# Gated cross-attention block: attention scores of three heads at once into three banks, one bank for transposed probabilities, four small loads moved to GpSimd's queue, and a new hand-written order of every engine

## The chip, the cores and the metric

One core of a Trainium2 chip runs the whole program. The metric is the device time of one execution in microseconds (us). The engines are TensorE (PE, with its weight loads shown apart as PEld), VectorE (DVE), ScalarE (ACT), GpSimd (POOL) and SyncE (SP), which only issues transfers.

## What is computed

Eight sequences of 256 rows by 512 channels go through a gated cross-attention and a gated feed-forward block. The attention has 16 heads of 32 channels, float32 scores, softmax and values; its two outer projections work on rows quantised to integers, and the feed-forward part on rows rounded to an 8-bit float.

```python
x = x + jnp.tanh(g_xattn[0]) * xattn(_layernorm(x, axis=-1), ctx_2048, mask, wq, bq, wk, bk, wv, bv, wo, bo)
...
# xattn: q = w8a8_linear(x, wq, bq); k = cond @ wk.T + bk; v = cond @ wv.T + bv
scores = jnp.einsum('bhnd,bhld->bhnl', q, k) * inv_sqrt_d + mask[:, None]
attn = jax.nn.softmax(scores, axis=-1)
o = jnp.einsum('bhnl,bhld->bhnd', attn, v)
return _w8a8_linear(o, wo, bo)
...
# ffn, on the layer-normed x: g, u = 8-bit linears with w_gate, w_up (1408 x 512)
t = jax.nn.silu(g) * u
y = 8-bit linear of t with w_down; the result is x + tanh(g_ffn[0]) * y
```

## The kernel before

The program is a software pipeline over eight batches. In each step three generations are worked at once: the attention of the last batch (heads 4 to 15 in slots 0 to 11, the first four heads of the new batch in slots 12 to 15), the projections K, V and Q of the new batch, and the output projection and feed-forward of the batch before. A step has 16 slots, one per head. Step 0 (`first_step_order`) and step 1 (`second_step_order`) also prepare the weights: wq, wk, wv, wo, and 15 "units" of the feed-forward weights, each scaled (`scale_unit`, DVE), lifted (`mag_unit`, ACT: an absolute value and a scaled copy), rounded (`round_unit`, DVE), transposed (`turn_unit`, PE) and copied out (`copy_unit`, ACT). Steps 2 to 7 are alike (`steady_step_order`). The tail (`tail_order`) ends the last attention (blocks `k`) and has two feed-forwards to do, the second of them (blocks `e`) on buffers of its own.

Every engine runs its own list of blocks in order; the lists are written out by hand, and semaphores hold the engines together. So what comes behind a block that waits on an engine waits too.

The path of one head: `score_pair` (L797) on PE writes the scores of two heads into `S_BANK[0]` and `S_BANK[1]`, one 512-column PSUM bank each. A head has 32 channels, so its matmuls use 32 rows of the array, each head of a pair another 32, and the two heads' matmuls alternate (L804 to L807). `head_mask` (L1292, DVE) adds the mask and takes the row's extremum into `prob` (two buffers); `head_exp` (L603, ACT) exponentiates in place; `head_turn` (L865, PE) transposes the 256 x 256 probabilities of the head of the slot before into one of two `T_BANK`s; `head_probT` (L617, ACT) copies that to `probT`; and after four heads `group_pv` (L900, PE) multiplies with V into bank O. `head_turn` waits for the exponentials (`exped`) and for the copy of the head two before (`turned_out`). `score_pair` waits until both heads before it are masked (L803). The eight calls per step score slots in pairs.

At the turn of a step: `oqT_turn` (L876, PE) transposes the rounded attention output, `oqT_low` (L1285, DVE) and `oqT_high` (L563, ACT) copy it out of PSUM, and `y_project` (L1003, PE) needs both. `v_evac(12)` (L1329 and `v_out`, L1219, DVE) moves the second half of V out of bank O (`V_BANK[1]`), and `group_pv(13)` waits for it (`v_ready`) since it writes that bank.

Loads: SP issues wq, wk, x, the context, wv, then two gates, two bias rows, wo, and the bias columns bk and bq (L303 to L312), and then the mask. ACT's `gate_tanhs` (L549) waits for all four small loads (`small_loaded` at 64), and everything behind it on ACT with it. GpSimd gathers gate and up rows by index (`load_unit`, L328).

## Time and profile before

| | us |
|---|---|
| median of 3 runs | 603.62 |
| lowest and highest of them | 601.6, 651.39 |
| the profiled execution | 601.54 |
| its span, first to last instruction | 599.8 |

The rows below are from the profiled execution. They are its page (a summary by engine and by group of instructions) and answers of its trace: timelines, tables of stretches, and lists of waits. "L807" is line 807 of the kernel. Matmuls are pipelined, and their ends are modelled: what a group of matmuls costs is read from its start to the start of the next group. DVE and ACT instructions overlap by up to 0.1 us in the timelines in the same way.

### The profile page before, as it was taken

The page shows a single profiled execution, that of the slowest core. Times are in us where ns is not written, and L with a number is a line of the kernel's source. Part 1 is how long each engine was busy: PE and PEld are TensorE (multiplying, and loading weights), DVE is VectorE, ACT ScalarE, POOL GpSimd, SP SyncE. Part 2 cuts the span into 40 slices and gives each one's busy share as a digit, 9 for nine tenths or more (in the row PEclk, how much of TensorE's full clock was granted, in tenths as well). Part 3 has the DMA queues.
Part 4 walks back from the last instruction along what each step waited for, and adds up shares of the span by engine and source line. Part 5 has one row for each costly group of instructions (what it writes and reads, how often), then busy time and mean ns, then how long its engine had stood idle before and what let it go on. Part 6 is the DMA issues. An engine that isn't in the chain of part 4 may idle for free.

```text
span 599.8 us, 10833 instructions
## 1 busy us (share of the span) xinstructions
PE 524.7 (87%) x3456; PEld 331.9 (55%) x3456; DVE 514.4 (86%) x1286; ACT 475.6 (79%) x1156; POOL 225.6 (38%) x208
## 2 busy tenths in 40 slices
PE   1867897899999999999999999999999998876834
PEld 1755475556755675577557655765576555433311
DVE  5798997678899989998999799979997996699794
ACT  5298998989888889888988898889788987783351
POOL 3223343002472447244715471546164613361430
PEclk9886997989999999999999999999999998796888
DMA  9912433010101010101010101010100000000000
GB/s 315 342 45 54 122 107 105 18 54 2 37 0 55 36 37 2 54 36 37 2 54 37 37 0 55 37 36 1 54 37 1 1 2 36 0 2 0 35 1 36
DMA packets 15240, 28.75 MB, mean 48 GB/s; under 512 B 3792, under 2 KB 5840, under 8 KB 15184
## 3 DMA queue, kind: packets, MB, share of 16 engines
q1 hardware_dynamic: 10560, 16.65, 8.1%
q0 software_dynamic: 3200, 11.41, 5.7%
q8 instruction: 28, 0.46, 0.3%
q10 hardware_dynamic: 1424, 0.01, 0.1%
q14 instruction: 28, 0.23, 0.1%
HBM read 23.87 MB, written 4.19 MB: 47 GB/s over the span
## 4 chain that ended last, share of the span: by engine, by line
PE 55%; DVE 23%; issue 10%; ACT 5%; SPq 3%; DMA 2%; DVEq 0%; POOL 0%; POOLq 0%; ACTq 0%
PE bank_s L807 9%; PE bank_t L872 7%; PE bank_u L827 5%; PE bank_g L827 5%; PE bank_a L814 4%; PE bank_g L814 4%; DVE prob L1299 3%; PE bank_o L914 3%; DVE q L1194 3%; PE bank_a L838 3%; DVE t_sb L1189 2%; DMA bq_col<-in_L_xattn_bq_dram 2%; DVE t_sb L1233 2%; DVE ts L1484 2%; PE bank_g L1048 2%
## 5 line engine op out<-in xcount | busy, mean ns | idle before, releaser
L612 ACT ACTIVATE prob<-prob,neg_max 128x256 f32<-128x256 f32 x256 | 127.2, 503 | 2.8 <-DVE neg_max L1299 2.8
L1299 DVE CUSTOM_DVE_ANT_0 prob<-bank_s,mask_sb 128x256 f32<-128x256 f32 x256 | 96.4, 420 | 19.9 <-PE bank_t L872 9.2
L623 ACT ACTIVATE probT<-bank_t 128x512 f32<-128x512 f32 x128 | 73.2, 588 | 20.2 <-PE bank_t L872 17.3
L397 POOL TENSOR_TENSOR up<-up,wgu_scale 128x512 f32<-128x512 f32 (+1 forms) x42 | 54.8, 1305 | 88.9 <-ACT up L592 88.9
L872 PE MATMUL bank_t<-ident,prob 128*128 128x128 f32 x512 | 78.3, 281 | 3.0 <-ACT prob L612 2.6
L807 PE MATMUL bank_s<-kf,qf 32*128 32x256 f32 x512 | 74.3, 408 | 6.9 <-DVE neg_max L1299 4.7
L872 PEld LDWEIGHTS bank_t<-ident,prob 128*128 128x128 f32 x512 | 59.2, 143 | 30.1 <-issue 19.7
L807 PEld LDWEIGHTS bank_s<-kf,qf 32*128 32x128 f32 x512 | 44.6, 188 | 31.0 <-issue 19.6
L407 POOL TENSOR_TENSOR up<-gate,up 128x512 f32<-128x512 f32 (+1 forms) x42 | 54.4, 1295 | 4.1 <-DVE gate L1359 1.4
L412 POOL TENSOR_TENSOR x<-x,y 128x512 f32<-128x512 f32 x14 | 19.6, 1399 | 96.6 <-DVE y L1497 96.6
L612 ACT ACTIVATION_READ_ACCUMULATOR prob<-prob,neg_max 128x1 f32 x256 | 50.1, 196 | 0.0
L827 PE MATMUL bank_u<-wguT,x2T 128*128 128x512 bf16 (+1 forms) x168 | 41.2, 369 | 0.0
L827 PE MATMUL bank_g<-wguT,x2T 128*128 128x512 bf16 (+1 forms) x168 | 40.6, 364 | 0.0
L1359 DVE SCALAR_TENSOR_TENSOR gate<-bank_g,x2s,wgu_scale 128x512 f32<-128x512 f32 (+1 forms) x42 | 29.5, 703 | 11.6 <-PE bank_g L827 11.6
L914 PE MATMUL bank_o<-probT,v_sb 128*32 128x256 f32 x512 | 36.0, 401 | 3.1 <-ACT probT L623 3.0
L513 ACT ACTIVATE mag<-t_sb,ts 128x512 f32<-128x512 f32 (+1 forms) x42 | 28.6, 681 | 11.1 <-DVE ts L1489 5.6
L592 ACT ACTIVATE up<-bank_u,x2s 128x512 f32<-128x512 f32 (+1 forms) x42 | 27.0, 643 | 6.4 <-PE bank_u L827 5.5
L1233 DVE SCALAR_TENSOR_TENSOR t_sb<-th,up 128x512 f32<-128x512 f32 (+1 forms) x42 | 30.5, 727 | 1.2 <-POOL up L407 1.2
L814 PE MATMUL bank_a<-c_in,wkT 128*128 128x256 f32 x128 | 31.4, 390 | 0.0
L679 ACT ACTIVATE th<-gate 128x512 f32<-128x512 f32 (+1 forms) x42 | 24.8, 589 | 8.3 <-DVE gate L1359 7.7
L820 PE MATMUL bank_a<-wvT,c_in 128*128 128x512 f32 x64 | 31.2, 610 | 0.0
L820 PE MATMUL bank_o<-wvT,c_in 128*128 128x512 f32 x64 | 30.5, 602 | 0.0
(258 smaller groups left out, 1213.8 us busy)
## 6 DMA issues: line engine op xcount, KB each, us to landing
x_in<-in_x_dram SPq DMA_DIRECT2D x8, 512.0 KB
c_in<-in_ctx_dram SPq DMA_DIRECT2D x8, 512.0 KB, 3.4
out_dram<-x POOLq DMA_DIRECT2D x7, 512.0 KB, 3.3
mask_sb<-in_mask_BxSxS_ff_dram SPq DMA_DIRECT2D x8, 256.0 KB, 3.7
t_sb<-in_L_ffn_w_down_dram SPq DMA_DIRECT2D x2, 704.0 KB, 5.3
t_sb<-in_L_ffn_w_down_dram POOLq DMA_DIRECT2D x2, 704.0 KB
kf<-in_L_xattn_wq_dram SPq DMA_DIRECT2D x1, 1024.0 KB, 8.9
probT<-in_L_xattn_wk_dram SPq DMA_DIRECT2D x1, 1024.0 KB, 11.0
```

The costliest lines, as they stand in the source:

```text
L397: pool.tensor_tensor(up[:, c % 2, 0:w], up[:, c % 2, 0:w], wu_scale[:, off:off + w], ALU.mult).then_inc(f["u_scaled"], 1)
L407: pool.tensor_tensor(up[:, c % 2, 0:w], gate[:, c % 2, 0:w], up[:, c % 2, 0:w], ALU.mult).then_inc(f["gu_ready"], 1)
L612: ins = act.activation(prob[:, head_par, t, :], prob[:, head_par, t, :], ACT.Exp, bias=neg_max[:, head_par, t:t + 1], scale=-1.0, accum_ou ...
L623: act.activation(probT[:, (slot + 3) % 4, :, :].rearrange("p a b -> p (a b)"), T_BANK[(slot + 1) % 2][:, :], ACT.Copy).then_inc(s["turned_ ...
L807: ins = pe.matmul(S_BANK[(slot + i) % 2][:, t * L:(t + 1) * L], qf[r:r + 32, hb, c, t * P:(t + 1) * P], kf[r:r + 32, hb, c, :], start=(t = ...
L814: ins = pe.matmul(k_bank(W, hf)[:, o * L:(o + 1) * L], wkT[:, c, (2 * hf + o) * P:(2 * hf + o + 1) * P], ctxT(c), start=(c == 0), stop=(c ...
L820: ins = pe.matmul(V_BANK[lt][:, :], ctxT(c)[:, lt * P:(lt + 1) * P], wvT[:, c, :], start=(c == 0), stop=(c == CC - 1))
L827: ins = pe.matmul(bk_[:, 0:w], x2T[:, c, t * P:(t + 1) * P], wT[:, c, off:off + w], start=(c == 0), stop=(c == CC - 1))
L872: ins = pe.transpose(T_BANK[1 - hp][:, lc * N + t * P:lc * N + (t + 1) * P], prob[:, 1 - hp, t, lc * P:(lc + 1) * P], ident[:, :])
L914: ins = pe.matmul(O_BANK[32 * j:32 * j + 32, 0:N], v_sb[:, 1 - par, lc, (4 * g + j) * Dh:(4 * g + j + 1) * Dh], probT[:, j, lc, :], start= ...
L1233: dve.scalar_tensor_tensor(t_sb[t][:, off:off + w], th[:, 0:w], 1.0, up[:, c % 2, 0:w], ALU.add, ALU.mult).then_inc(f["t_ready"], 1)
L1299: ins = dve.tensor_tensor_reduce(prob[:, hp, t, :], S_BANK[hp][:, t * L:(t + 1) * L], mask_sb[:, hb, t, :], -1.0, 3.4e38, ALU.add, ALU.min ...
```

## The change

- `S_BANK` has three banks and `T_BANK` one. `score_group` scores three heads with interleaved matmuls at four places of a step (called from slots 2, 5, 8 and 15) and two at two places (slots 11 and 13): six groups for 16 heads where there were eight.
- `head_turn` waits for the copy of the head right before it, as there is one bank.
- SP no longer issues the two gates, bk and bq; wo follows wv at once. GpSimd issues those four ahead of its first gather.
- For units 7, 9, 11 and 13 the scaled copy of `mag_unit` goes from ACT to DVE (two `tensor_scalar` in `round_unit`).
- The order lists of PE, ACT and DVE are rewritten in all steps, GpSimd's in steps 0 and 1 and in the tail. Among them, in the steady step: on PE no score group stands between `oqT_turn` and `y_project`, but `head_turn(1)`; `group_pv(13)` follows `first_score(11)` at once; on ACT `head_exp(0)` and `head_probT(0)` stand ahead of `oqT_high`; on DVE `v_evac(12)` stands behind `head_mask(12)`.

```diff
-        S_BANK, T_BANK, O_BANK, A_BANK, G_BANK, U_BANK = bank[0:2], bank[2:4], bank[4], bank[5], bank[6], bank[7]
+        S_BANK, T_BANK, O_BANK, A_BANK, G_BANK, U_BANK = (bank[0], bank[1], bank[3]), bank[2], bank[4], bank[5], bank[6], bank[7]
+        SCORED_FROM = {2: 3, 5: 3, 8: 3, 11: 2, 13: 2, 15: 3}
+        SCORE_BANK = [S_BANK[slot % 3] for slot in range(12)] + [S_BANK[0], S_BANK[1], S_BANK[2], S_BANK[0]]
...
-            return (S_BANK + T_BANK)[e % 4]
+            return bank[e % 4]
...
+        DVE_UNITS = (7, 9, 11, 13)
...
                     load8("v", wv)
-                    for n, g in enumerate((g_xattn, g_ffn)):
-                        sp.dma_start(gates[:, n:n + 1], g.rearrange("(a n) -> a n", a=1).to_broadcast([P, 1])).then_inc(s["small_loaded"], 16)
+                    load8("o", wo)
                     sp.dma_start(bo_row[:, :], bo.rearrange("(a n) -> a n", a=1).to_broadcast([P, C])).then_inc(s["row_loaded"], 16)
                     sp.dma_start(bv_row[:, :], bv.rearrange("(a n) -> a n", a=1).to_broadcast([P, C])).then_inc(s["row_loaded"], 16)
-                    load8("o", wo)
-                    sp.dma_start(bk_col[:, :], bk.rearrange("(c p) -> p c", p=P), allow_slow_non_contiguous=True).then_inc(s["small_loaded"], 16)
-                    sp.dma_start(bq_col[:, :], bq.rearrange("(c p) -> p c", p=P), allow_slow_non_contiguous=True).then_inc(s["small_loaded"], 16)
                     sp.wait_ge(s["wq_loaded"], 16)
...
+            for n, g in enumerate((g_xattn, g_ffn)):
+                pool.dma_start(gates[:, n:n + 1], g.rearrange("(a n) -> a n", a=1).to_broadcast([P, 1])).then_inc(s["small_loaded"], 16)
+            pool.dma_start(bk_col[:, :], bk.rearrange("(c p) -> p c", p=P), allow_slow_non_contiguous=True).then_inc(s["small_loaded"], 16)
+            pool.dma_start(bq_col[:, :], bq.rearrange("(c p) -> p c", p=P), allow_slow_non_contiguous=True).then_inc(s["small_loaded"], 16)
             pool.wait_ge(s["index_loaded"], 16)
             load_unit(2)
             load_unit(3)
@@ -419,10 +422,10 @@
                     load, x_var, x2_add, x2_var, x_plus_bias, up_scale, gate_up, out_add, out_store)
 
             def first_step_order(k):
-                k.load(4); k.x_var(0); k.load(6); k.x_plus_bias(4); k.load(8); k.load(12); k.load(10); k.load(14)
+                k.x_var(0); k.load(6); k.load(4); k.load(8); k.x_plus_bias(4); k.load(10); k.load(14); k.load(12)
 
             def second_step_order(k):
-                k.load(0); k.load(4); k.x_plus_bias(4); k.x_var(0); k.load(2); k.load(8); k.load(6)
+                k.load(0); k.load(4); k.x_plus_bias(4); k.load(2); k.x_var(0); k.load(6); k.load(8)
...
                     for n in range(2):
-                        act.activation(m[:, n * C:(n + 1) * C], raw[:, n * C:(n + 1) * C], ACT.Abs, scale=wf_r[:, k % 3, 1, n:n + 1])
-                    for n in range(2):
+                        ins = act.activation(m[:, n * C:(n + 1) * C], raw[:, n * C:(n + 1) * C], ACT.Abs, scale=wf_r[:, k % 3, 1, n:n + 1])
+                    for n in range(0 if k in DVE_UNITS else 2):
                         ins = act.activation(raw[:, n * C:(n + 1) * C], raw[:, n * C:(n + 1) * C], ACT.Copy, scale=wf_r[:, k % 3, 0, n:n + 1])
...
-                                   T_BANK[(slot + 1) % 2][:, :], ACT.Copy).then_inc(s["turned_out"], 1)
+                                   T_BANK[:, :], ACT.Copy).then_inc(s["turned_out"], 1)
...
             def first_step_order(k):
...
+                k.unit_mag_0(0); k.unit_mag(2); k.pro_round_q(0); k.x_centre(0); k.pro_k(0); k.ctxT_copy(0)
+                k.ctxT_copy(1); k.pro_round_o(3); k.unit_mag(4); k.gate_tanhs(2); k.k_out_0(3); k.k_out_1(4)
+                k.x_round(2); k.pro_v(2); k.unit_copy(3); k.wo_scaled(6); k.unit_mag(6); k.xT_high(6); k.unit_copy(5)
+                k.unit_copy(7); k.unit_mag(8); k.unit_copy(9); k.unit_mag(10); k.q_high(7); k.unit_copy(11)
+                k.q_high(8); k.unit_mag(12); k.head_exp(12); k.head_exp(13); k.head_probT(13); k.unit_copy(13)
+                k.unit_mag(14); k.head_exp(14); k.head_probT(14); k.head_exp(15); k.unit_copy(15); k.head_probT(15)
 
...
+                k.head_exp(0); k.head_probT(0); k.oqT_high(0); k.head_exp(1); k.ctxT_copy(0); k.x_centre(0)
+                k.group_oT(1); k.head_probT(1); k.ctxT_copy(1); k.head_exp(2); k.head_probT(2); k.x_round(2)
+                k.head_probT(3); k.head_exp(3); k.head_probT(4); k.k_out_0(3); k.head_exp(4); k.x2_mag_0(3)
+                k.x2_mag_1(3); k.group_oT(5); k.head_exp(5); k.head_probT(5); k.k_out_1(4); k.head_probT(6)
...
+                k.head_exp(10); k.head_probT(10); k.gate_tanh(11); k.head_exp(11); k.head_probT(11); k.head_probT(12)
+                k.tT_high(12); k.t_mag_0(12); k.head_exp(12); k.t_mag_1(12); k.t_mag_2(13); k.head_exp(13)
+                k.head_probT(13); k.group_oT(13); k.tT_high(14); k.head_probT(14); k.head_exp(14); k.head_exp(15)
+                k.head_probT(15); k.o_round(15)
...
-                def score_pair(slot):
+                def score_group(slot, count):
 
                     n = 16 * b + slot - LEAD
                     h = (slot + 4) % SLOTS
                     hb = 1 - par if slot < LEAD else par
 
-                    need(pe, s["masked"], n)
+                    need(pe, s["masked"], n - 1 if slot in (LEAD, LEAD + 2) else n)
                     for t in range(NT):
-                        for i in range(2):
+                        for i in range(count):
                             c, r = (h + i) // 4, 32 * ((h + i) % 4)
-                            ins = pe.matmul(S_BANK[(slot + i) % 2][:, t * L:(t + 1) * L], qf[r:r + 32, hb, c, t * P:(t + 1) * P],
+                            ins = pe.matmul(SCORE_BANK[(slot + i) % SLOTS][:, t * L:(t + 1) * L], qf[r:r + 32, hb, c, t * P:(t + 1) * P],
                                             kf[r:r + 32, hb, c, :], start=(t == 0), stop=True, skip_group_check=True)
                             if t == NT - 1:
                                 ins.then_inc(s["scored"], 1)
...
-                    need(pe, s["turned_out"], n - 2)
+                    need(pe, s["turned_out"], n - 1)
                     for lc in range(LC):
                         for t in range(NT):
-                            ins = pe.transpose(T_BANK[1 - hp][:, lc * N + t * P:lc * N + (t + 1) * P],
+                            ins = pe.transpose(T_BANK[:, lc * N + t * P:lc * N + (t + 1) * P],
                                                prob[:, 1 - hp, t, lc * P:(lc + 1) * P], ident[:, :])
                     ins.then_inc(s["turned_ps"], 1)
...
-                k.head_score(15)
+                k.pro_turn_k(0); k.pro_turn_q(0); k.ctxT_turn(0); k.ctxT_turn(1); k.k_project_even(2)
+                k.k_project_even(3); k.unit_turn(2); k.k_project_odd(2); k.k_project_odd(3); k.pro_turn_v(1)
+                k.wo_scale_turn(5); k.xT_turn(4); k.unit_turn(4); k.pro_turn_o(4); k.xT_turn(5); k.sx_turn(6)
+                k.unit_turn(6); k.q_project_0(6); k.unit_turn(8); k.q_project_1(7); k.unit_turn(10)
+                k.v_project_low(10); k.v_project_high(10); k.first_score(11); k.v_project_low(11); k.head_turn(13)
+                k.unit_turn(12); k.head_score(13); k.head_turn(14); k.v_project_high(11); k.head_score(15)
+                k.unit_turn(14); k.head_turn(15)
...
-                k.head_turn(0); k.ctxT_turn(0); k.oqT_turn(0); k.head_score(1); k.y_project(0); k.head_turn(1)
-                k.head_turn(2); k.ctxT_turn(1); k.group_pv(1); k.k_project_even(2); k.head_score(3); k.head_turn(3)
-                k.k_project_odd(2); k.head_turn(4); k.k_project_even(3); k.xT_turn(4); k.group_pv(5)
-                k.k_project_odd(3); k.xT_turn(5); k.head_turn(5); k.head_score(5); k.x2T_turn(5); k.sx_turn(6)
-                k.head_turn(6); k.up_project(5); k.gate_project(5); k.q_project_0(6); k.up_project(6)
-                k.gate_project(6); k.head_turn(7); k.up_project(7); k.head_score(7); k.gate_project(7); k.head_turn(8)
-                k.up_project(8); k.q_project_1(7); k.gate_project(8); k.up_project(9); k.head_score(9); k.head_turn(9)
-                k.gate_project(9); k.group_pv(9); k.up_project(10); k.v_project_low(10); k.gate_project(10)
-                k.v_project_high(10); k.head_turn(10); k.v_project_low(11); k.first_score(11); k.head_turn(11)
-                k.head_turn(12); k.tT_turn(11); k.v_project_high(11); k.down_project_low(12); k.head_score(13)
-                k.down_project_high(12); k.group_pv(13); k.head_turn(13); k.tT_turn(13); k.head_turn(14); k.o_turn(14)
-                k.down_project_low(14); k.down_project_high(14); k.head_turn(15); k.head_score(15)
+                k.head_turn(0); k.ctxT_turn(0); k.oqT_turn(0); k.head_turn(1); k.y_project(0); k.group_pv(1)
+                k.ctxT_turn(1); k.head_score(2); k.head_turn(2); k.k_project_even(2); k.head_turn(3)
+                k.k_project_odd(2); k.head_turn(4); k.k_project_odd(3); k.xT_turn(4); k.k_project_even(3)
+                k.group_pv(5); k.head_turn(5); k.head_score(5); k.sx_turn(6); k.x2T_turn(5); k.head_turn(6)
+                k.xT_turn(5); k.up_project(5); k.gate_project(5); k.up_project(6); k.head_turn(7); k.q_project_0(6)
+                k.gate_project(6); k.up_project(7); k.q_project_1(7); k.gate_project(7); k.head_turn(8)
+                k.up_project(8); k.gate_project(8); k.head_score(8); k.head_turn(9); k.group_pv(9); k.up_project(9)
+                k.gate_project(9); k.v_project_low(10); k.v_project_high(10); k.up_project(10); k.gate_project(10)
+                k.v_project_low(11); k.head_turn(10); k.v_project_high(11); k.head_turn(11); k.tT_turn(11)
+                k.head_turn(12); k.first_score(11); k.group_pv(13); k.down_project_low(12); k.down_project_high(12)
...
+                if k in DVE_UNITS:
+                    for n in range(2):
+                        dve.tensor_scalar(raw[:, n * C:(n + 1) * C], raw[:, n * C:(n + 1) * C], wf_r[:, k % 3, 0, n:n + 1], None,
+                                          ALU.mult).then_inc(s["wf_lifted"], 1)
+                    dve.wait_ge(s["wf_lifted"], 2 * DVE_UNITS.index(k) + 2)
...
             def first_step_order(k):
...
+                k.pro_int_q(0); k.x_scales(2); k.pro_q(0); k.pro_scale_o(2); k.unit_scale(2); k.unit_round(3)
+                k.unit_scale(4); k.unit_round(5); k.pro_v(2); k.pro_int_o(4); k.bias_scale(3); k.xT_low(5); k.pro_o(5)
+                k.sx_copy(7); k.unit_scale(6); k.unit_round(7); k.q_scale_0(7); k.unit_scale(8); k.unit_round(9)
+                k.q_scale_1(8); k.unit_scale(10); k.unit_round(11); k.v_evac(11); k.head_mask(12); k.head_mask(13)
+                k.unit_round(13); k.unit_scale(12); k.head_mask(14); k.head_mask(15); k.unit_scale(14); k.v_evac(12)
+                k.unit_round(15)
...
             def steady_step_order(k):
                 k.head_mask(0); k.head_mask(1); k.oqT_low(0); k.x_stats(0); k.y_scale(1); k.head_mask(2)
...
+                k.x_scales(2); k.head_mask(3); k.x2_stats(2); k.x2_centre(3); k.head_mask(4); k.x2_max(3); k.xT_low(5)
+                k.head_mask(5); k.x2_sum_0(4); k.x2_sub_0(4); k.x2_sum_1(4); k.x2_sub_1(4); k.x2T_copy(5)
+                k.head_mask(6); k.gate_scale(6); k.head_mask(7); k.sx_copy(7); k.head_mask(8); k.q_scale_0(7)
+                k.gate_scale(7); k.t_mul(7); k.q_scale_1(8); k.gate_scale(8); k.t_mul(8); k.gate_scale(9); k.t_mul(9)
+                k.head_mask(9); k.t_scales(9); k.t_mul(10); k.gate_scale(10); k.t_sum_0(10); k.head_mask(10)
+                k.t_sub_0(10); k.t_sum_1(10); k.t_mul(11); k.t_sub_1(10); k.v_evac(11); k.gate_scale(11)
+                k.t_sum_2(11); k.head_mask(11); k.t_mul_last(11); k.t_sub_2(11); k.t_scales(11); k.head_mask(12)
+                k.v_evac(12); k.tT_low(12); k.t_sum_0(12); k.head_mask(13); k.t_sub_0(12); k.t_sum_1(12)
                 k.t_sub_1(12); k.t_sum_2(13); k.y2_scale(13); k.t_sub_2(13); k.head_mask(14); k.tT_low(14)
```

## Rows read from the trace of the kernel before

**Rows 1.** Parts 1 and 5 of the page: busy us and share; then busy, mean ns.

```profile
PE 524.7 (87%) x3456; PEld 331.9 (55%) x3456; DVE 514.4 (86%) x1286; ACT 475.6 (79%) x1156; POOL 225.6 (38%) x208
...
L623 ACT ACTIVATE probT<-bank_t 128x512 f32<-128x512 f32 x128 | 73.2, 588 | 20.2 <-PE bank_t L872 17.3
```

**Rows 2.** Table of stretches: window, length, then busy us of each engine, clock, DMA.

```profile
0.00:31.16 31.16, 14.85 (x85) 13.29 (x85) 20.94 (x36) 13.13 (x17) 8.32 (x18) 0.95 0.90 320
31.16:74.70 43.54, 31.43 (x189) 22.53 (x191) 39.15 (x76) 40.09 (x79) 13.83 (x12) 0.80 0.26 73
74.70:139.84 65.14, 55.39 (x397) 39.39 (x393) 51.69 (x138) 59.69 (x147) 12.01 (x12) 0.92 0.21 65
...
317.42:376.61 59.19, 58.96 (x403) 37.02 (x401) 53.80 (x148) 51.40 (x133) 26.36 (x24) 1.00 0.09 32
...
540.00:600.00 60.00, 33.80 (x152) 14.55 (x152) 46.63 (x82) 19.15 (x33) 14.54 (x12) 0.78 0.05 18
```

**Rows 3.** Timeline of PE in one steady step: start us, us, line, tile, count.

```profile
283.40 0.81 PE L827 MATMUL bank_u<-wguT,x2T 128*128 128x384 bf16 x4
284.14 1.13 PE L807 MATMUL bank_s<-kf,qf 32*128 32x256 f32 x8
285.20 0.82 PE L827 MATMUL bank_g<-wguT,x2T 128*128 128x384 bf16 x4
285.87 0.60 PE L872 MATMUL bank_t<-ident,prob 128*128 128x128 f32 x4
...
292.51 1.07 PE L914 MATMUL bank_o<-probT,v_sb 128*32 128x256 f32 x16
293.51 0.82 PE L827 MATMUL bank_u<-wguT,x2T 128*128 128x384 bf16 x4
```

**Rows 4.** Timeline of all engines at the turn of a steady step.

```profile
316.00 1.34 ACT L638 ACTIVATE rows<-rows,os 128x512 f32<-128x512 f32 x2 [1.12 <-DVE os L1352]
...
318.41 1.13 PE L807 MATMUL bank_s<-kf,qf 32*128 32x256 f32 x8
...
318.52 0.69 DVE L1290 TENSOR_SCALAR turned<-bank_g 128x512 bf16<-128x512 f32 x1 [0.36 <-PE bank_u L884]
319.01 0.50 ACT L612 ACTIVATE prob<-prob,neg_max 128x256 f32<-128x256 f32 x1
...
319.48 1.04 PE L1008 MATMUL bank_u<-woT,turned 128*128 128x512 bf16 x4
```

**Rows 5.** Timeline of DVE: a head's mask, and V leaving bank O.

```profile
303.73 0.42 DVE L1299 CUSTOM_DVE_ANT_0 prob<-bank_s,mask_sb 128x256 f32<-128x256 f32 x1
...
307.65 0.68 DVE L1223 TENSOR_TENSOR v_sb<-bank_o,bv_row 128x512 f32<-128x512 f32 x1
```

**Rows 6.** Timeline of ACT, and of DVE, in step 0: the two late loads.

```profile
31.16 0.20 ACT L551 ACTIVATE tgate<-gates 128x2 f32<-128x2 f32 x1 [10.68 <-DMA bq_col<-in_L_xattn_bq_dram]
30.26 2.29 DVE L1132 TENSOR_REDUCE w_max<-raw_o 128x4 f32<-128x2048 f32 x1 [3.21 <-DMA raw_o<-in_L_xattn_wo_dram]
```

**Rows 7.** DMA issues of the page: KB each, us from issue to landing.

```profile
qf<-in_L_xattn_wv_dram SPq DMA_DIRECT2D x1, 1024.0 KB, 15.4
raw_o<-in_L_xattn_wo_dram SPq DMA_DIRECT2D x1, 1024.0 KB, 18.1
```

**Rows 8.** Timeline of SP's queue: when it issued.

```profile
5.18 1.46 SPq L286 DMA_DIRECT2D qf<-in_L_xattn_wv_dram  x1
...
12.17 0.52 SPq L286 DMA_DIRECT2D raw_o<-in_L_xattn_wo_dram  x1
...
17.23 4.79 SPq L312 DMA_DIRECT2D bq_col<-in_L_xattn_bq_dram  x1
```

**Rows 9.** Groups of ACT's and DVE's unit work: busy us, mean ns.

```profile
L1420 DVE TENSOR_SCALAR rows<-x,mv 128x512 f32<-128x512 f32 x14 | 6.2, 484 | 0.2
...
L476 ACT ACTIVATE t_sb<-t_sb,wf_r 128x512 f32<-128x512 f32 x8 | 5.4, 732 | 0.0
```

**Rows 10.** What ACT waited for from 31.2 to 139.9 us: total, times, longest.

```profile
ACT wguT L488 <- PE bank_g L787: 3.9, 4, 2.1
```

186 lines of the change are left out of this document (76 added, 110 removed).

## The prediction, made before the changed kernel ran

> **What bounds the kernel now.** I read the page first: PE is busy 87% of the span, DVE 86%, ACT 79% [rows 1]. Those are averages, so the table of stretches comes next [rows 2]. It shows three regimes. Steps 0 and 1, up to 139.84 us, are different: from 31.16 us on ACT is busy 40.09 of 43.54 and then 59.69 of 65.14 us, more than any other engine, so ACT carries them, and before that it stands still for 10.68 us until bq_col has landed [rows 2, 6]. From 540 us on DVE is busiest (46.63 of 60.00), in chains of short dependent work.
>
> I split 599.8 us into 139.84 (steps 0 and 1), 355.1 (six steps of 59.18) and 104.9 (the tail), and sum against the profiled execution, 601.54. The median shown, 603.62, is 2 us above it, the lowest run, 601.6, at it.
>
> **Steady steps: what the third head saves.** A pair costs 1.06 us from its start at 284.14 to the next group at 285.20 [rows 3]. Two heads of two halves each, in two passes per matmul, are eight records in four rounds. That the work of several heads runs side by side is seen in the product with V: sixteen records, four heads wide, take 1.00 us (292.51 to 293.51), no more than eight records of two. So I cost a group of three like a pair, 1.06; the far end is that the third head runs by itself, another 1.06 at most, since a lone head has the same four rounds. Six groups for eight save 2 x 1.06 = 2.12. The block in front of a group is a little longer too: up_project of 384 columns takes 0.74 ahead of the scores, the same form 0.67 elsewhere (285.20 to 285.87), so two groups fewer give another 0.14. Sum: -2.26 a step. The Trainium skill, TensorEngine Tiling (Array Packing), Key Properties, says that changing the tiling mode drains TensorE and that different tiles may run in parallel; this trace agrees (0.07 us in front, pairs at 1.06), and without that drain the saving would be 2.12.
>
> **Steady steps: what the new order takes back.** I followed the new lists block by block with the old durations. Three places stand out.
> (a) `oqT_turn` to `y_project`. Before, a score group (318.41 to 319.48) filled exactly the time that DVE (318.52 + 0.69) and ACT needed to copy the transposed rows [rows 4]. Now only `head_turn(1)`, about 0.45, stands there, and ACT does `head_exp(0)` and `head_probT(0)` ahead of `oqT_high`: from the end of `o_round` at 317.34, 2 x 0.49 for the exponentials and 0.48 for the copy end at 318.9, `oqT_high` at 319.5, so `y_project` starts at 319.6, where it did. PE loses the score's 1.06 less 0.45: +0.6.
> (b) `group_pv(13)` needs `v_evac(12)`, which now stands behind `head_mask(12)` on DVE, which needs `first_score(11)`, the block right in front of `group_pv(13)` on PE. PE must stand still for the mask (2 x 0.35), the evacuation (0.61 net of overlap) and two handovers of 0.1 [rows 5]: +1.5 in each step, whatever else is on time. Down projection, `o_turn` and the next step are queued behind it.
> (c) `head_score(2)` waits for `head_mask(2)`, behind `y_scale`: +0.15.
> Against that, today's list too holds waits too short for the lists of waits, and where PE stands anyway, these cost nothing more; I estimate -0.5. Net: -2.26 + 0.6 + 1.5 + 0.15 - 0.5 = -0.5 to -0.7. I take **-0.6 a step, -3.6 for six**. Ends: -2.26 (nothing lost, -13.6) and +0.5 (the lost time twice as long as I see, +3).
>
> **One T bank.** A turn now waits for the copy of the head before it. The copy takes 0.588 [rows 1], with handovers 0.75. In the steady list PE has at least the eleven transposes of `tT_turn` between any two turns and nearly always over 1 us, and ACT's list has each copy near its turn. I cost it 0.1 a step, inside the sum above; if half of the turns were uncovered by 0.7, it would be +5.6 a step.
>
> **Steps 0 and 1.** (d) The stall. `gate_tanhs` waited for bq_col until 31.16 [rows 6]; SP issued it at 17.23, as its last [rows 8]. Now GpSimd issues the four from about 2 us. If each took the longest time that SP needed for one, 4.79, the last would be issued at 16.4, and with the 13.9 from issue to the end of ACT's wait, land at 30.3. On ACT's new list `gate_tanhs` comes behind `pro_round_o` and `unit_mag(4)`, about 32, so that wait is gone even so. GpSimd's gathers of units 2 and 3 would then start at 21 at the latest, and are first read at 27: covered. What is late next is wo: `pro_round_o` now stands ahead. wo was issued at 12.17 and took 18.1, landing at 30.26 [rows 6 to 8]. It is now issued at 6.7, behind wv, which landed at 5.18 + 15.4 = 20.6; 1 MB at the stretch's 320 GB/s [rows 2] is 3.3 more, so 24 to 25 with the gathers beside it. DVE's maximum (2.29 + 0.4) ends at 27.6, and ACT then goes on with the same work done as at 31.16: **-3.5**. The Trainium skill, DMA: Bandwidth & Descriptors, Issuing engine by pattern, calls the sync and scalar paths generally faster for simple loads; no run here shows GpSimd's time for such a load, and by the bounds above it changes nothing.
> (e) The offload. Four units of two copies, 0.61 net of overlap each (0.73 shown [rows 9]), leave ACT: -4.9 on the engine that carries these steps. DVE gets eight of 0.40 net (0.484), 3.2 us; it is busy 39.15 of 43.54 and 51.69 of 65.14, so the second stretch has 13 us for them [rows 2]. **-4.9**.
> (f) Order. After 31.2 ACT still waited, mostly for `unit_turn` and `copy_unit` (3.9 [rows 10]). Walking the new lists I find `o_round` of step 1 ending at about 128 for 139.8, which is 3.3 more than (d) and (e). A walk forgets small waits; I take half: **-1.6**.
> Together -10; bounds -3.5 (the offload only moves the bound to DVE) and -12.
>
> **Tail.** `up_project(5)` comes some 2 us earlier by my walk, but `group_pv(13)` and `o_turn` some 2 later, as they stand behind all gate and up projections, and from 540 DVE's own list sets the end. 0, within +-3.
>
> **Sum.** 601.5 - 3.6 - 10.0 + 0 = 588.
>
> **The rivals.**
> 1. The steady step keeps all that the third head saves: PE is as full as before, and (a) to (c) do not show. For it: PE's 58.96 of 59.19. Against: (b) is forced by the lists. 601.5 - 13.6 - 10 = 578.
> 2. Only the offload or only the early wo counts in steps 0 and 1, and the steady step is a draw: DVE, 2 x 3.2 us nearer to full, or the later `ctxT_turn` becomes the bound. For it: DVE is within 1 us of ACT until 74.7 us. 601.5 - 4.5 + 1 = 598.
> 3. On the other side: the third head doesn't ride along. Price: 1.06 for each of four groups of three, +4.2 a step on PE, which has no slack, some 1 us of it absorbed: -0.6 + 3.2 = +2.6 a step, and 4 in the other steps: 601.5 - 10 + 16 + 4 = 612. It decides from 1.6 us for a group of three, where all gains are eaten. For it: the trace has no three row groups at once. Against: four column groups at 1.00.
> 4. The lone T bank at the price above: +33, 621. Against: no turn stands next to another in the steady list of PE.
>
> **Chances.** Forecast (588, own range 582 to 595) 0.50; rival 1 0.20; rival 2 0.18; rival 3 0.07; rival 4 0.05. The range of 576 to 600 holds the first three but for their outer ends, and about 0.8. A measurement here can tell about 2%, 12 us: faster by over that means below 591.5 against 603.6: all of rival 1 and 0.42 of the forecast's 0.50, 0.62. Slower by over 2%, above 615: rival 4 and part of rival 3, 0.08. Between: 0.30.
>
> **What would show it.** Right: 12 records of scores in about 1.07 us from start to start; a PE gap of 1.3 to 1.6 us ahead of `group_pv(13)` in each steady step with DVE's mask and V in it; steady steps of 58.3 to 58.8 us; ACT with no wait at `tgate`, one for wo's scale ending at 27 to 28; `oqT_turn` of step 2 near 130. Wrong: groups of three over 1.3 us; steps under 57.3 or over 59.2; probabilities' turns waiting for ACT's copy over 1 us a step; bq_col landing after 32; step 2 starting after 136.

## The result, and the profile after

The changed kernel is slower: 616.33 us (median of 4 runs) against 604.91 for the kernel before on the same chips, a ratio of 1.0218 (95% interval 1.0155 to 1.0282). One run of the kernel before, a slow one of 651.39 us, is in its median but not in the ratio. The change is slower beyond the noise; whether by more than 2%, the interval leaves open. The profiled execution spans 614.5 us, the one before 599.8. In the same three parts as in the prediction (cut at the start of `oqT_turn` on TensorE):

| us | before | after | difference | forecast |
|---|---|---|---|---|
| steps 0 and 1 | 139.84 | 137.10 | -2.7 | -10.0 |
| six steady steps | 355.1 (59.18 each) | 367.4 (60.5, then 61.3 to 61.7) | +12.3 | -3.6 |
| tail | 104.9 | 110.0 | +5.1 | 0 |

Part 1 of the page after, and two groups of part 5. They answer to [rows 1]: TensorE is busy 7 us less, but 6.6 of that is in steps 0 and 1 (101.7 to 95.1), where its mean granted clock was 0.97 and not 0.89; in the six steady steps, with twelve groups of scores fewer, it is busy only 1.7 us less (353.5 to 351.8). ScalarE's copy of the turned probabilities waits 37.7 us for TensorE (17.3 before).

```profile
PE 517.3 (84%) x3456; PEld 322.2 (52%) x3456; DVE 519.3 (85%) x1294; ACT 473.9 (77%) x1148; POOL 225.7 (37%) x212
...
L626 ACT ACTIVATE probT<-bank_t 128x512 f32<-128x512 f32 x128 | 75.9, 593 | 38.8 <-PE bank_t L875 37.7
...
L917 PE MATMUL bank_o<-probT,v_sb 128*32 128x256 f32 x512 | 39.3, 430 | 14.7 <-DVE v_sb L1229 9.9
```

The last row has the loss in it: the product with V waited 9.9 us for V to leave its bank, and its matmuls have a mean of 430 ns (401 before). The table of stretches after (columns as in [rows 2]): steps 0 and 1, then a steady step.

```profile
31.16:74.70 43.54, 33.71 (x229) 24.60 (x228) 36.82 (x71) 35.18 (x71) 13.83 (x14) 0.96 0.39 116
74.70:137.10 62.40, 50.69 (x400) 36.51 (x398) 55.98 (x146) 58.80 (x145) 12.34 (x12) 0.96 0.20 62
...
320.26:381.92 61.66, 58.90 (x403) 36.28 (x401) 54.22 (x148) 51.82 (x133) 26.16 (x24) 0.97 0.09 31
```

The steady step has the busy time of [rows 2] (58.90 against 58.96) though TensorE has less to do, and a granted clock of 0.97, not 1.00. The timeline of TensorE after shows why: first a group of three, then the place ahead of `group_pv(13)`.

```profile
325.95 0.48 PE L810 MATMUL bank_s<-kf,qf 32*128 32x256 f32 x2
...
327.02 0.66 PE L875 MATMUL bank_t<-ident,prob 128*128 128x128 f32 x4
...
364.98 1.13 PE L810 MATMUL bank_s<-kf,qf 32*128 32x256 f32 x8
367.77 1.85 PE L917 MATMUL bank_o<-probT,v_sb 128*32 128x256 f32 x16 [1.65 <-DVE v_sb L1229]
369.56 2.32 PE L1051 MATMUL bank_g<-wdT,turned 128*128 128x512 bf16 x6
371.72 1.24 PE L1057 MATMUL bank_g<-wdT,turned 128*128 128x512 bf16 x5
...
376.73 1.46 PE L1051 MATMUL bank_g<-wdT,turned 128*128 128x512 bf16 x6
378.02 0.60 PE L875 MATMUL bank_t<-ident,prob 128*128 128x128 f32 x4
```

Three heads take 1.07 us from start to start (325.95 to 327.02), as a pair does [rows 3]: the third head rides. Ahead of V TensorE stands still for 1.65 us, and what follows is slow: the product takes 1.79 (367.77 to 369.56; 1.00 in [rows 3]), the down projection 2.16 (to 371.72; 1.29 for the same six matmuls at 376.73). The table of stretches shows the clock of that place: at the 2.4 GHz level up to the pause, near the 1.2 GHz level (0.52 of full in the mean; 0.50 from 368.5 to 371.3) behind it.

```profile
364.00:367.70 3.70, 2.12 (x21) 1.42 (x18) 3.02 (x10) 2.89 (x8) 0.00 (x0) 1.00 0.59 215
367.80:371.20 3.40, 3.40 (x20) 1.25 (x21) 3.37 (x9) 2.68 (x6) 0.00 (x0) 0.52 0.02 5
```

The pause stands in all six steady steps, 1.65 us each time, but the low clock in five of them. In the first steady step the same pause was followed by work at full clock:

```profile
185.36 1.07 PE L917 MATMUL bank_o<-probT,v_sb 128*32 128x256 f32 x16 [1.65 <-DVE v_sb L1229]
186.36 1.47 PE L1051 MATMUL bank_g<-wdT,turned 128*128 128x512 bf16 x6
```

VectorE's timeline at the pause: the mask waits for the scores that stand right ahead of the pause, and V leaves its bank behind it.

```profile
366.24 0.42 DVE L1305 CUSTOM_DVE_ANT_0 prob<-bank_s,mask_sb 128x256 f32<-128x256 f32 x1 [0.61 <-PE bank_s L810]
...
366.94 0.69 DVE L1229 TENSOR_TENSOR v_sb<-bank_o,bv_row 128x512 f32<-128x512 f32 x1
```

And the turn of the step, TensorE and ScalarE after: the place of [rows 4]. `head_turn(1)` waits 0.75 us for ScalarE's copy; `y_project` (L1011) then starts at 322.54, when ScalarE's other copy has ended (321.82 + 0.58).

```profile
321.82 0.58 ACT L571 ACTIVATE turned<-bank_u 128x512 bf16<-128x512 f32 x1
322.05 0.63 PE L875 MATMUL bank_t<-ident,prob 128*128 128x128 f32 x4 [0.75 <-ACT probT L626]
322.54 1.02 PE L1011 MATMUL bank_u<-woT,turned 128*128 128x512 bf16 x4
```

The books of a steady step with the low clock in it, from start to start of TensorE's blocks: 59.2 before; -2.1 for two groups fewer; +1.65 pause ahead of V; +0.79 and +0.87 slow work behind it; +0.75 at the turn of the step; +0.1 elsewhere: 61.3. The first steady step has no slow work and took 60.5; some 0.7 of it is not explained by these terms, and a_v_first's first steady step is 0.7 longer than its typical one, too.

### The profile page after: what moved, and what is told of

Its sections match the earlier page's. It is cut to its first block, busy times and chain, and to the rows that moved or that the text cites. A ratio compares the mean times of both kernels' runs of the same rounds, so it can differ in the third digit from the quotient of the medians.

```text
span 614.5 us, 10833 instructions
## 1 busy us (share of the span) xinstructions
PE 517.3 (84%) x3456; PEld 322.2 (52%) x3456; DVE 519.3 (85%) x1294; ACT 473.9 (77%) x1148; POOL 225.7 (37%) x212
## 4 chain that ended last, share of the span: by engine, by line
PE 57%; ACT 14%; DVE 12%; issue 10%; POOL 3%; DMA 3%; SPq 0%; POOLq 0%; ACTq 0%; DVEq 0%
PE bank_t L875 8%; PE bank_s L810 6%; PE bank_o L917 5%; PE bank_u L830 5%; PE bank_a L817 4%; ACT prob L615 4%; PE bank_g L817 3%; PE bank_g L830 3%; PE bank_g L1051 3%; ACT probT L626 2%; DVE prob L1305 2%; ACT t_sb L517 2%; PE bank_a L841 2%; PE bank_g L1057 2%; DMA kf<-in_L_xattn_wq_dram 2%
## 5 line engine op out<-in xcount | busy, mean ns | idle before, releaser
L626 ACT ACTIVATE probT<-bank_t 128x512 f32<-128x512 f32 x128 | 75.9, 593 | 38.8 <-PE bank_t L875 37.7
L875 PE MATMUL bank_t<-ident,prob 128*128 128x128 f32 x512 | 82.9, 286 | 15.4 <-ACT probT L626 13.7
L400 POOL TENSOR_TENSOR up<-up,wgu_scale 128x512 f32<-128x512 f32 (+1 forms) x42 | 51.1, 1216 | 87.2 <-ACT up L595 87.2
L1305 DVE CUSTOM_DVE_ANT_0 prob<-bank_s,mask_sb 128x256 f32<-128x256 f32 x176 | 66.7, 420 | 10.4 <-PE bank_s L810 4.1
L410 POOL TENSOR_TENSOR up<-gate,up 128x512 f32<-128x512 f32 (+1 forms) x42 | 57.4, 1366 | 5.3 <-DVE gate L1365 2.5
L810 PE MATMUL bank_s<-kf,qf 32*128 32x256 f32 x352 | 55.2, 406 | 1.8 <-DVE neg_max L1305 1.8
L917 PE MATMUL bank_o<-probT,v_sb 128*32 128x256 f32 x512 | 39.3, 430 | 14.7 <-DVE v_sb L1229 9.9
L810 PE MATMUL bank_t<-kf,qf 32*128 32x256 f32 x160 | 46.0, 407 | 0.0
L810 PEld LDWEIGHTS bank_s<-kf,qf 32*128 32x128 f32 x352 | 33.1, 187 | 16.2 <-issue 10.8
L1305 DVE CUSTOM_DVE_ANT_0 prob<-bank_t,mask_sb 128x256 f32<-128x256 f32 x80 | 30.6, 420 | 4.9 <-PE bank_t L875 4.3
L917 PEld LDWEIGHTS bank_o<-probT,v_sb 128*32 128x32 f32 x512 | 15.2, 117 | 30.8 <-issue 20.7
```

The costliest lines, as they stand in the source:

```text
L400: pool.tensor_tensor(up[:, c % 2, 0:w], up[:, c % 2, 0:w], wu_scale[:, off:off + w], ALU.mult).then_inc(f["u_scaled"], 1)
L410: pool.tensor_tensor(up[:, c % 2, 0:w], gate[:, c % 2, 0:w], up[:, c % 2, 0:w], ALU.mult).then_inc(f["gu_ready"], 1)
L626: act.activation(probT[:, (slot + 3) % 4, :, :].rearrange("p a b -> p (a b)"), T_BANK[:, :], ACT.Copy).then_inc(s["turned_out"], 1)
L810: ins = pe.matmul(SCORE_BANK[(slot + i) % SLOTS][:, t * L:(t + 1) * L], qf[r:r + 32, hb, c, t * P:(t + 1) * P], kf[r:r + 32, hb, c, :], st ...
L875: ins = pe.transpose(T_BANK[:, lc * N + t * P:lc * N + (t + 1) * P], prob[:, 1 - hp, t, lc * P:(lc + 1) * P], ident[:, :])
L917: ins = pe.matmul(O_BANK[32 * j:32 * j + 32, 0:N], v_sb[:, 1 - par, lc, (4 * g + j) * Dh:(4 * g + j + 1) * Dh], probT[:, j, lc, :], start= ...
```

## The experiments

The starts of `oqT_turn` cut every run into the same parts. The ratio is to the kernel before, on the same chip. The same lists and loads of steps 0 and 1 gave 135.2 to 137.1 in four kernels (after, a_v_first, a_filled, a_v_half), and 133.8 to 135.7 in five with late small loads. The kernel before spreads more: b_half has its lists, loads and code in steps 0 and 1 unchanged and took 136.2 where before took 139.84. In b_half the granted clock from 31.16 to 74.7 us was 0.88, in before 0.80:

```profile
31.16:74.70 43.54, 29.63 (x189) 20.74 (x191) 39.77 (x76) 39.83 (x79) 14.38 (x12) 0.88 0.26 75
```

So a difference to before of under 4 us in that column is no finding by itself; there the ratios of the whole, from many runs, decide. "Typical" is the middle of the steady steps: the first two of a_v_first took 59.9 and 60.4, and one of a_tlow 61.2.

| kernel | ratio, 95% interval | steps 0, 1 | a steady step (typical) |
|---|---|---|---|
| after | 1.0218 (1.0155, 1.0282) | 137.1 | 61.3 |
| a_v_first | 1.0015 (0.9984, 1.0045) | 137.0 | 59.1 |
| a_filled | 1.0098 (1.0063, 1.0133) | 135.2 | 59.7 |
| a_turn | 1.0472 (1.0423, 1.0521) | 137.1 | 63.0 |
| mixed | 1.0067 (1.0020, 1.0114) | 137.8 | 60.0 |
| a_v_half | 0.9968 (0.9924, 1.0012) | 135.7 | 59.2 |
| b_half | 0.9939 (0.9894, 0.9983) | 136.2 | 58.8 |
| a_best | 0.9968 (0.9927, 1.0009) | 134.3 | 59.2 |
| a_tlow | 1.0056 (1.0007, 1.0105) | 135.7 | 59.5 |
| a_tlow_half | 0.9972 (0.9917, 1.0026) | 134.4 | 59.2 |
| a_mask13b | 1.0250 (1.0206, 1.0293) | 133.8 | 61.5 |
| a_mask13 | 1.0294 (1.0252, 1.0335) | 134.2 | 61.5 |
| b_loads | 0.9964 (0.9933, 0.9996) | 138.6 | 59.2 |
| b_loads_late | 0.9928 (0.9895, 0.9960) | 135.0 | 59.2 |
| b_offload | 1.0050 (1.0011, 1.0089) | 143.7 | 59.2 |
| a_first_old | 1.0270 (1.0216, 1.0323) | 138.3 | 61.3 |
| a_second_old | 1.0552 (1.0505, 1.0599) | 156.1 | 61.3 |
| a_no_offload | 1.0339 (1.0280, 1.0398) | 143.8 | 61.3 |

**The pause and its clock.** a_v_first moves one block of the changed kernel:

```diff
-k.t_scales(11); k.head_mask(12); k.v_evac(12); k.tT_low(12)
+k.t_scales(11); k.v_evac(12); k.head_mask(12); k.tT_low(12)
```

> The changed kernel with one block of VectorE moved in the steady steps: V's second half leaves bank O (v_evac(12)) ahead of the mask of slot 12 instead of behind it. In the changed kernel TensorE stands still for 1.65 to 1.8 us ahead of group_pv(13) in each steady step, and for 3.4 us behind that its granted clock is 0.50, so that the product with V takes 1.79 to 1.85 instead of 1.00 and the first down projection 2.16 instead of 1.29. Theory 1 (this wait and the clock that falls behind it are the main loss of the steady steps): the gap falls to about 0.4 us, the clock stays at 1.00, and a step goes from 61.3 to 58.0-58.4 us; six steps give back 18 us: 596-599. Theory 2 (only the wait counts; the work behind it waits for something else anyway): 59.7 a step, -10 us, 605-607. Theory 3 (VectorE's masks and the exponentials of slots 12 and 13 are what is late): 61 a step, no change.

59.1 a step: between theories 1 and 2. The timeline of TensorE in a_v_first at the same place:

```profile
303.39 1.07 PE L917 MATMUL bank_o<-probT,v_sb 128*32 128x256 f32 x16 [0.24 <-DVE v_sb L1229]
304.71 1.47 PE L1051 MATMUL bank_g<-wdT,turned 128*128 128x512 bf16 x6 [0.25 <-DVE turned L1333]
...
308.25 0.66 PE L875 MATMUL bank_t<-ident,prob 128*128 128x128 f32 x4
309.62 0.28 PE L1044 MATMUL bank_g<-ident_h,q 128*128 128x128 bf16 x2 [0.71 <-DVE q L1200]
```

The granted clock is 1.00 in all six steady steps. Of the 3.3 us of pause and slow clock 0.24 is left; another 0.25 + 0.71 come back where TensorE now waits for VectorE's next results. That leaves 2.1 of a gain, and 2.2 were measured. a_filled leaves the pause's cause and only fills it:

```diff
+def warm(slot):
+    for i in range(14):
+        pe.transpose(S_BANK[2][:, (i % 4) * P:(i % 4 + 1) * P], ident[:, :], ident[:, :])
...
-k.first_score(11); k.group_pv(13)
+k.first_score(11); k.warm(13); k.group_pv(13)
```

> The changed kernel with 14 more transposes of a constant (about 1.5 us of TensorE work whose result nobody reads), put into the gap ahead of group_pv(13) in each steady step. Nothing else is moved, and the wait for V stays. If the fallen clock has a price of its own, group_pv(13) and the down projection behind it run at full speed although TensorE got more work: 0.8 + 0.87 = -1.6 us a step, 59.6-59.8, and 606-608 for the whole. If the low clock costs nothing (what stands behind waits for other engines anyway), the step stays at 61.3 and the time at 616; if the extra work doesn't fit the gap, it is longer by what sticks out, some 0.2 us a step.

Measured as theory 1 says: 59.7 a step. TensorE did more, had V no sooner, and the step was 1.6 us shorter. TensorE's timeline in a_filled (here L1055 is the first down projection), and a row of its table of stretches with the clock:

```profile
301.16 1.75 PE L933 MATMUL bank_t<-ident 128*128 128x128 f32 x14
302.88 1.07 PE L917 MATMUL bank_o<-probT,v_sb 128*32 128x256 f32 x16
303.89 1.47 PE L1055 MATMUL bank_g<-wdT,turned 128*128 128x512 bf16 x6
305.19 1.24 PE L1061 MATMUL bank_g<-wdT,turned 128*128 128x512 bf16 x5
```

```profile
302.00:306.00 4.00, 4.00 (x35) 2.17 (x34) 3.96 (x12) 3.29 (x9) 0.00 (x0) 1.00 0.05 15
```

The first steady step is a control: there the clock had not fallen, and the filler gained nothing (60.47 against 60.48). So the pause costs twice where the clock falls: 1.65 us itself, 1.6 us by the clock behind it, 8.1 us over the steady steps (367.4 against 359.3). The Trainium skill, TensorE: Matmul & The Clock Gate, HAM oscillation, describes a loop in which TensorE waits for a transfer in each pass and starts the next one cold. The loss here is of that kind, at a pause of 1.65 us, shorter than the waits shown there.

The length of a pause alone does not decide. a_turn (below) has two pauses of 1.65 us and more in every steady step, and its granted clock stayed at 1.00 through all six; a_tlow has one of 1.39 in each, and the clock fell behind it in the second step only. What decides, no run here shows.

**The loads.** b_loads is the kernel before with the changed loads alone; b_loads_late issues GpSimd's four behind its gathers.

> The kernel before with the changed loads alone: the two gates, bk and bq by GpSimd's queue, wo directly behind wv. Theory 1 (my step d): ScalarE's wait of 10.7 us for bq_col goes; its gate comes at about 22.5 when the K projection and the copies let it, then it waits for wo, which lands near 26 as in the changed kernel; step 2's output transposes start at 136-137 instead of 139.84, the whole 3 to 3.5 us faster. Theory 2 (wq and wk, which landed 2 us later in the changed kernel, are late because of the moved transfers): they land at 11 and 13 us after issue here too, and take 2 us of that: 1 to 1.5 us faster. Theory 3: the wait only moves on to TensorE and VectorE: no change.

> The kernel before with the changed loads, but GpSimd issues the four small ones behind its first four gathers, near 17 us, instead of at 2 us. With them at 2 us, wq and wk landed 10.9 and 12.9 us after issue instead of 8.9 and 11.0, and step 2's output transposes started at 138.56 (139.84 before). Theory 1: the small transfers, 2 us each of tiny pieces, stand in the way of wq and wk; behind the gathers they don't, wq and wk land after 8.9 and 11.0 again, and step 2 starts 2 us earlier, at 136.5; the whole is 3.3 us faster than before. Theory 2: wo behind wv (4 MB in flight at once) slows wq and wk: they land late here too, and it stays at 138.5. If the gates then land after 29 us, ScalarE waits for them and the gain is lost.

b_loads: theory 2, 1.3 us in steps 0 and 1 (the whole: 0.4%, or 2 us). b_loads_late: theory 1, 4.9 us in steps 0 and 1 (the whole: 0.7%, or 4.3 us, with an interval of 2.4 to 6.3). When wq and wk landed is the firmer evidence. Two DMA issues of b_loads, then of b_loads_late (KB, us to landing):

```profile
kf<-in_L_xattn_wq_dram SPq DMA_DIRECT2D x1, 1024.0 KB, 11.0
probT<-in_L_xattn_wk_dram SPq DMA_DIRECT2D x1, 1024.0 KB, 13.1
```

```profile
kf<-in_L_xattn_wq_dram SPq DMA_DIRECT2D x1, 1024.0 KB, 8.6
probT<-in_L_xattn_wk_dram SPq DMA_DIRECT2D x1, 1024.0 KB, 10.7
```

The four small transfers, issued by GpSimd from 2 us on, were what made wq and wk late; wo behind wv was not. With them issued from 16.6 us on ScalarE waited 4.95 us for bq_col (10.68 before [rows 6]). This kernel, the old one with a few lines moved, is the fastest of all: 598.62 us, 0.9928.

**Offload and lists of steps 0 and 1.** b_offload is the kernel before with `DVE_UNITS` alone, a_no_offload the changed kernel with `DVE_UNITS = ()`; a_first_old and a_second_old put the old lists of one step back into the changed kernel.

> The kernel before with the offload alone: the scaled copy of units 7, 9, 11 and 13 on VectorE (eight operations of 0.48) and not on ScalarE (eight of 0.73, 0.61 net). My step e: ScalarE carries steps 0 and 1, so step 2's output transposes start 4.9 us earlier than 139.84, at 135, and the whole takes 4.9 less. Rival 1: VectorE's rounding was as late as ScalarE; each lifted unit comes 0.8 us later to its rounding and TensorE's unit transposes with it: no gain, 139-140. Rival 2: half, since ScalarE waits for TensorE and VectorE in these steps in any case: 137.5.

> The changed kernel with the scaled copies of units 7, 9, 11 and 13 back on ScalarE; everything else as changed. In the old lists the offload alone made step 2 start 3.8 us later (143.65 against 139.84), since VectorE's roundings came later. Theory 1: that holds for the new lists too: without the offload step 2's output transposes start at 135-136 instead of 137.1, the whole 614-615. Theory 2: the new lists were made for the offload, ScalarE carries step 1 in them (58.8 us busy of 62.4), and without it they start up to 4.9 us later: 140-142, the whole 619.

> The changed kernel with the lists of step 0 of all four engines as they were before (V's first half leaves its bank one place earlier than there, ahead of the mask of slot 15); loads, offload, three-head scores and all other steps stay as changed. Theory 1: in the changed kernel the new order of step 0 eats what the loads and the offload give, because the context's transposes stand behind wq's on TensorE and the K projection starts at 27.96 us instead of 22.36. Then the K projection starts at about 24.4 (wk lands 2 us later than before), ScalarE's gate comes at about 27, the first scores 5 us earlier than 63.2, and the first transposition of step 2's output starts at 133-134 instead of 137.1: the whole 612-613. Theory 2: steps 0 and 1 are bound by step 1's order or by the work itself; the gain of step 0 is lost in waits of step 1: 136.5-138, the whole 615-617.

> The changed kernel with the lists of step 1 of all four engines as they were before, fitted to groups of three and to one T bank (score groups at slots 2, 5, 8, the last ahead of the Q projection; the context's two transposes next to each other; the copies of the turned probabilities in ascending order). With step 0's old lists the changed kernel was no faster (138.3 us to step 2's output transposes, against 137.1), so what ate the gain of loads and offload must be looked for in step 1. Theory 1: step 1's new order does it; with the old one the transposes start at 133-134 us and the whole takes 613. Theory 2: it is the single T bank together with ScalarE as the bound of this step (turns wait for copies: 3.8 + 3.7 us in the stretch); then it is 137 or later whatever the order, as the old order has its turns in closer pairs: 137-140, 616-619.

b_offload: rival 1, and worse, +3.8 (up to 1.3 of it is wo, which landed that much later in its profile; the whole is 0.5% or 3 us slower, with an interval of 0.7 to 5.4). Yet in the new lists the same offload is worth 6.7 us (143.8 against 137.1; the ratios, 1.0339 and 1.0218, say 7). An order list and the durations it was written for belong together; an edit's value can't be carried from one list to the other. a_first_old: theory 2; the new list of step 0 is not what eats the gain. a_second_old is far worse, 19 us. Pairs of turns close to each other now share one T bank there; the list of waits of a_second_old from 74.7 to 134 us:

```profile
PE bank_t L875 <- ACT probT L626: 7.6, 4, 3.1
ACT probT L626 <- PE bank_t L875: 7.2, 5, 4.1
DVE prob L1305 <- PE bank_t L875: 6.9, 4, 4.3
```

Three engines wait for each other around one bank. In the changed kernel the first of these rows reads 3.8 in the same stretch, and in before no turn of probabilities waits for a copy; VectorE's wait for that bank (the third row) is there too, at 6.1. This points to a price of the lone bank in step 1, most of which the new lists avoid, but doesn't show it: the old lists were also fitted to groups of three. One bank alone was not tried in the old lists: they can't hold it, since ScalarE copies the second half of the context ahead of `head_probT(1)`, and TensorE turns head 2 ahead of `ctxT_turn(1)`. How the 7 us missing in steps 0 and 1 split among bank, groups and lists stays open; against b_half's 136.2 nothing was gained in them at all.

**The turn of a step.** a_turn is a_v_first with the scores of slots 0 to 2 between `oqT_turn` and `y_project`, and ScalarE's and VectorE's copies of the transposed rows first. `head_turn(1)` and `head_score(2)` moved back in TensorE's list too, and the exponentials of slots 0 and 1 in ScalarE's. Pieces of TensorE's list:

```diff
-k.down_project_high(14); k.head_score(15)
+k.down_project_high(14)
...
-k.head_turn(0); k.ctxT_turn(0); k.oqT_turn(0); k.head_turn(1); k.y_project(0); k.group_pv(1); k.ctxT_turn(1); k.head_score(2)
+k.head_turn(0); k.ctxT_turn(0); k.oqT_turn(0); k.head_score(-1); k.y_project(0); k.group_pv(1); k.ctxT_turn(1); k.head_turn(1)
```

> The changed kernel with V leaving its bank ahead of the mask of slot 12 (59.1 us a step), and in addition the turn of a step as it was in kind: the group of three scores of slots 0 to 2 is not the last of a step but stands between oqT_turn and y_project, and ScalarE copies the transposed rows before the exponentials of slots 0 and 1. Theory 1: TensorE's idle 0.75 us at the turn goes, as the scores (1.07) cover the copies of VectorE and ScalarE: 58.4 a step, 598-599 for the whole. Theory 2: the masks and exponentials of slots 0 to 2, which now come 2.5 us later, become what TensorE's turns wait for: the gap only moves, 59.1 or more, 603 or slower.

Theory 2, much worse: 63.0. Its TensorE waits at other places:

```profile
264.13 0.65 PE L887 MATMUL bank_g<-ident,rows 128*128 128x128 f32 x4 [1.01 <-ACT rows L641]
...
271.80 0.48 PE L817 MATMUL bank_a<-c_in,wkT 128*128 128x256 f32 x1 [1.66 <-ACT c_in L537]
```

A third wait, of 1.66 us, stands at 279.28 ahead of a turn of probabilities, for ScalarE's exponentials: the one that theory 2 names. The group of scores at the end of the step had hidden the scaling and rounding of the attention output ahead of `oqT_turn` (the first wait, 1.01). With six groups there is one cover for two latencies in these lists; the two waits of 1.66 are for work of ScalarE that now comes later.

**What is left in the steady step.** With V first, TensorE has 2.1 us less work than before and the step is no shorter. mixed joins steps 0 and 1 of b_loads_late, steady steps of a_v_first with `gate_project(5)` ahead of `up_project(5)`, and the changed tail with `down_project_high(14)`, `y2_scale(15)` and GpSimd's adds ahead of the second feed-forward.

> A kernel of both. Steps 0 and 1 as before (pairs of scores, two score banks, two T banks, old lists, no offload), with the changed loads and the small ones issued behind GpSimd's first four gathers (134.96 us to step 2's output transposes in that run). Steady steps as changed (three score banks, one T bank), with V leaving its bank ahead of the mask of slot 12 (59.1 us a step in that run) and gate_project(5) ahead of up_project(5), so that VectorE's first gate_scale, for which it waited 1.3 us, starts 0.87 us earlier. The tail as changed, but the first feed-forward's last down projection, its scaling and GpSimd's adds stand ahead of the second feed-forward, as they did before. If VectorE's chain from x2T to the last quantised t is what TensorE waits for once its own wait is gone (0.93 at the second transposition of t, 0.3 and 0.3 near V), a steady step is 58.2-58.5 us; if TensorE's other waits (0.65 at the turn of a step) decide, 58.9-59.1. The tail behind the second oqT_turn takes 61.5 instead of 65.2 if those moved blocks are its cause. Sum: 135 + 6 x 58.3 + 44.8 + 61.7 = 591; with 59.1 a step 596. If the single T bank was not what made steps 0 and 1 slow in the changed kernel, they start step 2 at 138 or later here too.

The whole took 607.48 us, not 591 to 596. The tail: 54.9 us from the second `oqT_turn` to TensorE's last block, 57.2 in the changed kernel, 53.6 before. That looks as if the misplaced blocks were 2.3 of its 3.6, but a_best, with the same tail lists as mixed, took 56.8, and a_v_first, with the changed ones, 56.3. The mean granted clock behind the second `oqT_turn` was 0.80 in mixed, 0.74 in a_best and in the changed kernel, 0.78 before. The price of those blocks is not told from the clock. The gate first is a loss of 0.9 a step: `up_project(6)` then waited 0.78 for ScalarE to empty bank U. Steps 0 and 1 lost 2.3 us in a wait at the place where two banks turn into one, and so don't tell the price of the lone bank.

a_v_half and b_half cut the maximum in `t_scales` to `t_sb[t][:, 0:704]`.

> The changed kernel with V leaving its bank ahead of the mask of slot 12, and less work for VectorE: the maximum over a row of t (t_scales, 1.61 us each, two per steady step) is taken over its first 704 of 1408 columns only. That leaves out part of the computation; all other instructions stay. Theory 1 (with three-head groups TensorE has 2.1 us less to do than the kernel before, and what it waits for is now VectorE's chain, 54.2 us busy of 59.1): VectorE's 1.6 us less make the step shorter by about what TensorE waited ahead of and behind V and at the second transposition of t (0.3 + 0.3 + 0.9), so 57.6-58.3 instead of 59.13. Theory 2 (the waits left in the step are TensorE's and ScalarE's own order): 59.0-59.1.

> The kernel before with the same maximum over half of t's columns, which leaves out the same part of the computation. It tells whether VectorE bounded the steady steps before, too. My reading of the trace (TensorE busy 58.96 of 59.19 sets them alone): the step stays at 59.1-59.2. If VectorE's chain already stood behind TensorE there, 58.3-58.8. In the tail, where VectorE sets the end, both kernels should lose about 0.8 us for each of the two or more maxima on the path.

Both against my expectation: 59.17 (theory 2), and 58.81 for the old kernel, so VectorE had 0.37 us of a step in its hand even before, and the prediction's "PE alone sets the six steady steps" was not quite so. a_v_half's VectorE stood still just there:

```profile
302.02 0.42 DVE L1305 CUSTOM_DVE_ANT_0 prob<-bank_s,mask_sb 128x256 f32<-128x256 f32 x1 [0.76 <-PE bank_s L810]
...
302.71 0.69 DVE L1333 COPY turned<-bank_g 128x1024 bf16<-128x1024 bf16 x1
```

a_best takes the repairs together (V first, late small loads, the tail's blocks). a_tlow also has `tT_low(12)` ahead of `head_mask(12)`; a_tlow_half cuts the maximum too; a_mask13b and a_mask13 move `head_mask(13)` back, ahead of `t_sum_2(13)` and behind `t_sub_2(13)`.

> The changed kernel with what the runs so far showed to help, each in another stretch: V leaves its bank ahead of the mask of slot 12 in the steady steps (59.1 a step), the four small loads are issued behind GpSimd's first four gathers (wq and wk 2 us earlier), and in the tail the last down projection of the first feed-forward, its scaling and the adds stand ahead of the second feed-forward (2.3 us in the mixed kernel). Theory 1: the three add up: step 2's output transposes at 135, 6 x 59.2, 43.7 to the second oqT_turn and 62.5 behind it: 597-598, 0.99 of before, some 5 us better than with V alone. Theory 2: the new lists of steps 0 and 1, written for early small loads, don't use the earlier wq and wk (the context stands behind wq's transposes there): 137 stays, 600.

> The kernel with the three repairs (a_best, 59.17 us a steady step), and in the steady steps VectorE's copy of the transposed t (tT_low(12)) ahead of the mask of slot 12 instead of behind it. With VectorE relieved by 1.6 us (a_v_half) the step stayed at 59.17: VectorE then stood still for 0.76 us ahead of the mask of slot 12, which waits for the scores that TensorE does behind its transposes of t, and tT_low behind it held up TensorE's down projection by 0.79. Theory 1 (a second place of the kind of V: a mask that waits for late scores stands ahead of a copy that TensorE waits for): the wait between group_pv(13) and the down projection (0.3 here) goes, VectorE's chain to the second transposition of t starts 0.1 to 0.3 us earlier: 58.6-58.9 a step. Theory 2: with VectorE's full work the chain of 8.9 us from t_sub_2(11) to t_sub_2(13) is full in any order; what is gained at the down projection is waited for at the second transposition of t: 59.1.

> a_tlow (59.5 us a steady step, TensorE waits 1.6 us at the second transposition of t) with the maximum of t over half of its columns, which leaves out part of the computation: 0.8 us less in the chain between the two transpositions of t. With the mask of slot 12 ahead of tT_low the same cut gave nothing. Theory 1 (two bounds of about the same length, the chain's work and the mask that waits for late scores; each hides the other): with both taken away the wait at the second transposition of t falls from 1.6 to 0.8 and the step goes to 58.4-58.7. Theory 2 (something else holds TensorE there, the scale of y or ScalarE's magnitudes): 59.2-59.5.

> As a_tlow, and the mask of slot 13 stands ahead of t_sum_2(13), behind four of the roundings, instead of ahead of t_sub_0(12). It doesn't shorten the chain to the second transposition of t, it only gives ScalarE the exponential of slot 13 about 2.6 us later. Theory 1 (the order of the roundings counts: ScalarE's magnitudes for the next ones start earlier): 0.1 to 0.3 us less than a_tlow. Theory 2 (the chain is a sum of VectorE's work): the same as a_tlow.

> As a_tlow, but the mask of slot 13 stands behind the last rounding (t_sub_2(13)), out of the chain to the second transposition of t, the turn of the attention output (o_turn) ahead of head_turn(14) on TensorE, and the exponential of slot 13 behind the copy of oT on ScalarE. Theory 1 (VectorE's chain of 8.9 us between the two transpositions of t is what TensorE waits for, 0.93 us in the changed lists): 0.7 us leave the chain, 58.2-58.5 a step, 594-595 for the whole. Theory 2: exponential and turn of slot 13 come late now, and head_turn(14) waits for them as long: 59.1 or more.

a_best: theory 1 up to the tail (134.28, 59.2, 43.6 to the second `oqT_turn`), but 65.45 behind it where 62.5 were expected and the changed kernel took 65.15; the whole, 600.40 us, is not told from the kernel before (604.31 there). a_tlow: theory 2, the wait moved from the down projection to the second transposition of t. a_tlow_half: theory 2 again, TensorE still waits 1.35 us there (0.71 in a_v_first; its timeline first):

```profile
303.49 0.66 PE L875 MATMUL bank_t<-ident,prob 128*128 128x128 f32 x4
305.49 0.28 PE L1044 MATMUL bank_g<-ident_h,q 128*128 128x128 bf16 x2 [1.35 <-DVE q L1200]
```

```profile
297.98:305.49 7.51, 6.00 (x46) 3.10 (x48) 6.81 (x18) 7.17 (x18) 0.44 (x1) 1.00 0.24 88
```

The second fence is a row of its table of stretches, from ScalarE's copy behind `head_turn(12)` to the end of that wait: ScalarE busy 7.17 of 7.51 us and VectorE 6.81; the roundings of t go to and fro between them. Moving the mask of slot 13 back cost 2 us a step, both ways, where neither theory had a loss like that. In a_mask13b TensorE then waits 2.08 us at the second transposition of t and its clock falls behind that in five steps; in a_mask13 the clock fell in the first step only. So no single engine, wait or mask is the bound left; the runs show that it is neither VectorE's sum of work nor the mask ahead of `tT_low`, and they leave open whether ScalarE's part of that chain is.

## Why the prediction was wrong, point by point

- **The third head rides: right.** 1.07 us for three, six groups for eight, 2.1 us a step (forecast 2.26). Rival 3 is refuted.
- **(b), the wait of `group_pv(13)`: place right, price half.** Forecast 1.5, measured 1.65 and then, in five of six steps, 1.66 more, since TensorE's clock fell to 0.50 behind the pause. The step that failed is the term "+1.5 in each step": a pause of TensorE was priced by its length, with every block behind it at its old duration. It should have been +3.3 in those five. a_filled shows the two apart.
- **(a), the turn of the step: right.** Forecast +0.6, measured 0.75 of standing still; in a_turn, which moved a group there, other waits took its place.
- **(c)** is not seen as a wait of its own. **The slack of -0.5 is wrong:** nothing came back. Two slips of arithmetic stand beside it: the terms add to -0.51, not -0.6, and an end with "the lost time twice as long" is +1.2 a step, not +0.5.
- **One T bank, 0.1 a step: right in the steady step** (0.17 at `head_turn(14)`; the 0.75 at `head_turn(1)` would stand there anyway, as ScalarE's copy for `y_project` ends at 322.40). In step 1, where I gave it nothing, TensorE's turns waited 3.8 us for the copies; what that cost in the end is not shown. Rival 4 asked for waits in the wrong stretch.
- **(d), loads: half.** ScalarE's wait for bq_col went, and wo landed at 26.0 (forecast 24 to 25). What I missed is the other direction: I bounded when the small transfers would land, not what they would do to wq and wk, which were in flight at the time and landed 2 us later. 3.5 forecast, 1.3 measured (b_loads), 4.9 to be had (b_loads_late); by the ratios of the whole 2 and 4.3. The Trainium skill, DMA: Bandwidth & Descriptors, Issuing engine by pattern, leans against GpSimd for simple loads; here GpSimd issued each in 0.56 to 0.77 us, where SP took 4.79 for one [rows 8], and the price was paid by other transfers.
- **(e), the offload: the reasoning failed.** "It leaves the engine that carries these steps" needs a chain that runs on that engine. In the old lists it cost 3.8 us (3 by the ratio). As I read it, each unit's rounding on VectorE, its transposes and the heads queued behind them came later, but only part of that shows in the lists of waits. Only in lists written for it does it pay (6.7). (f) was a walk through lists with no waits in it and gave a start of 128 for 137. Its starting point, 139.84, was one execution; b_half's 136.2 for the same code shows how far that can be off.
- **Tail:** 0 within 3 forecast, +5.1 measured: 1.5 up to the second `oqT_turn`, the rest behind it. Of the 1.5, 1.3 is missing in a_filled, with the same tail lists (43.5 us for 44.9, at a mean granted clock of 0.92 for 0.88). How much of the rest is the last down projection and its scaling standing among the second feed-forward's chunks, and how much the clock, stays open.

In sum: -3.6 forecast for the steady steps against +12.3, of which the clock is 8; -10 against -2.7; 0 against +5.1. The steady steps are 15.9 us off, enough by themselves to turn the forecast gain into a loss, and 9.2 of that is the price of (b).

## What to carry to other kernels

Where a new order makes the fullest engine wait in every pass of a loop, look what runs behind the wait: on TensorE it can be not only the pause, but the work behind it at half clock. Before taking work off a full engine, list the latencies which that work was hiding, and count the covers that are left. Where a block that waits for late data (a mask for fresh scores) stands ahead of a short copy that another engine needs, try the copy first: it gave 2.2 us a step here for V, and nothing for the transposed t. Small transfers cost least here when nothing large and urgent was in flight. And before a part of a kernel is priced from one profile, see how far two executions of the same code differ in it.

## What the runs showed of the hardware

- Four loads of 5 KB in all, issued by GpSimd while 2 MB of weights were in flight on SP's queue, delayed these by 2 us; issued 14.5 us later they did not (11.0 and 13.1 us to landing against 8.6 and 10.7).
- Twelve records of score matmuls in three row groups take 1.07 us, about as long as eight in two (1.06).
- The same code of steps 0 and 1 took 139.84 and 136.2 us in two profiles, with mean granted clocks of 0.80 and 0.88 from 31.16 to 74.7 us.
